# Attention values in blocks of eight heads, with twelve probability slots, in a one-core decoder layer

## The chip, the cores and the metric

The kernel runs on one core of a Trainium2 chip. The metric is the device time of one execution in microseconds (us), as the median of three runs. Lower is better.

## The reference

The input is a batch of 16 sequences of 256 tokens with 256 features, a second sequence of the same shape (the context), and a mask that is all ones. Three sub-layers follow one another, each added to its input and normalised over the features:

```
q, k, v = x @ w_qkv.T        # 16 heads of 16 features
q, k = rope(rms_norm(q)), rope(rms_norm(k))
x = layernorm(x + softmax(causal(q k^T / 4)) v @ w_proj.T)      # self attention
x = layernorm(x + softmax(causal((x Wq)(ctx Wk)^T / 4)) (ctx Wv) @ Wo)   # cross attention
x = layernorm(x + light_ffn(x) + heavy_ffn(x))  # gelu networks of 128 and 1024 hidden units
```

The heavy network is routed to 256 tokens of a sequence, and a sequence has 256, so it reaches every token. All arithmetic is at fp32 precision; where operands are narrower they are split into two or three terms.

## The kernel before, in words

All five engines run an instruction stream of their own, written out by hand as a loop of steps `i` from -2 to 19, and wait for one another by semaphores. A step works on four batches at once: self attention of batch `s = i`, cross attention of `c = i - 1`, the end of cross attention of `f = i - 2`, and the feed-forward network of `l = i - 3`. A whole step in the middle of the run has four phases on TensorE (PE), each a loop over 16 heads (`phase`), with other work put ahead of a given head by a dictionary `others` (constants such as `V2_AT`, at the end of the file):

- S1, scores of self attention (`scores(1, s, h)`): VectorE (DVE) takes the row maxima of each head (L1048).
- S2, scores of cross attention (`scores(2, c, h)`), the same.
- T1, transposed scores of self attention (`scores_t(1, s, h)`): ScalarE (ACT) takes the exponential of each head into a slot of `pr` (L854), GpSimd (POOL) masks it (L1433), and PE multiplies it with the values.
- T2, the same for cross attention.

The scores of all four phases go through a ring of three PSUM banks: PE may write head `h` only when DVE or ACT has read head `h - 3`. From the fourth step on, most heads of S1 and S2 find the mask already in their bank, written there by ACT (`write_bias`, L788 `bank<-cmaskb`); for the others PE adds it by a matmul (`cmaskb,idb`).

The values are taken four heads at a time (`values(a, b, gr)`, `a` = 1 for self, 2 for cross attention). The four heads lie side by side in PSUM bank 3, 32 partitions each, in columns 0 to 255, and each consists of two fp32 matmuls (256 and 128 columns), each of which the trace shows as two records; so a group is 16 records, `bank<-pr,va`. ACT then copies the group to `oT` (`copy_group`, 128x256), and the next group waits for that copy. `pr` has eight slots, so the exponential of head 8 waits for the values of heads 0 to 3, and so on. Groups 0, 1 and 2 stand ahead of heads 7, 11 and 15 of their phase, group 3 ahead of head 3 of the next phase: in T2 for self attention, in S1 of the next step for cross attention.

What stands around the groups: in T1, nine feed-forward matmul pairs (`FFN1_AT`, heads 0 to 10) and the transposes of `xn` ahead of head 8; in T2, `k2` ahead of head 1, the two halves of `qk1` ahead of heads 3 and 6, the self attention's output projection ahead of head 9, `v1` ahead of head 13. From that projection comes the first layer norm: DVE adds and takes statistics, POOL takes the inverse deviation between its masks of heads 12 and 13 (`RSTD1_AT`, L1412), DVE writes `x` (L1135), and PE transposes `x` ahead of head 1 of S1 (`transpose_x1`). Behind it in S1: the last cross values ahead of head 3, `q2` ahead of head 4, then `out_tokens`, `out_dims`, the cross output projection and the hidden layer. In S2, the transposes of the rotated q and k stand ahead of head 2 (`transpose_qk1`), those of the maxima ahead of head 4, `v2` ahead of head 6 (`V2_AT`), the feed-forward output from head 3 on.

ACT's order in S2, which the prediction comes back to: load of the exponential's table, copies of the two transposed halves, `xThigh`, bias writes for heads 6, 7 and 8, the copy of `v2`, bias for head 9, the copy of the context, bias for heads 10 to 15.

The rotation of q and k reads `qn` (the normalised and scaled pair, written by `scale_qk` on DVE in S1) and writes `qr`, which PE transposes in the following S2.

Of the kernel before, what the change touches and what calls it, by code (L numbers as in the profile page):

```python
# [43 lines left out]
P = 128  # L44
# [12 lines left out]
NG = H // HG  # L57
NB = T // VW
# [7 lines left out]
def build(nc, io):  # L66
# [4 lines left out]
    with ctx:  # L71
# [38 lines left out]
        qn = sb("qn", [P, TT, 2 * D]); rot = sq; qc = sb("qc", [P, TT, 2 * D]); qr = sb("qr", [P, TT, 2 * D])  # L110
# [15 lines left out]
        pr = sb("pr", [P, 2 * HG, 3 * P])  # L126
# [91 lines left out]
        def iterations(step):  # L218
            for i in range(-2, B + 4):
# [3 lines left out]
                 if 0 <= turn[2] < B]  # L223
        RING = (0, 1, 2)
# [174 lines left out]
        def _(pe):  # L399
# [98 lines left out]
            def hidden(b, j):  # L498
# [11 lines left out]
                elif b == B - 2:  # L510
# [7 lines left out]
                    elif j == 6:  # L518
                        pe.wait_ge(s_y[3], b)
                    elif j == LIGHT:  # L520
                        pe.wait_ge(s_oT[2], NG * B)
# [8 lines left out]
                elif j == 1:  # L530
                    pe.wait_ge(s_oT[2], NG * (b + 2))
# [42 lines left out]
            def transpose_max(a, b):  # L574
# [3 lines left out]
                else:  # L578
                    if live(b - 3):
                        pe.wait_ge(s_g, FCH * (b - 3) + LIGHT)  # L580
                    if live(b - 2):
                        pe.wait_ge(s_oT[2], NG * (b - 1))
                    wait(pe, s_oT[1], NG * b)
# [14 lines left out]
            def values(a, b, gr):  # L598

                pe.wait_ge(s_prob[a], H * b + HG * (gr + 1))  # L600
                if gr == 0:
# [3 lines left out]
                    elif live(b + 1):  # L605
                        pe.wait_ge(s_oT[1], NG * (b + 2))
                    elif live(b - 2):
                        pe.wait_ge(s_g, FCH * (b - 1))
                else:
                    pe.wait_ge(s_oT[a], NG * b + gr)  # L610
                v = values_of(a, b)
                for key in range(2):
                    for j in range(HG):
                        h = HG * gr + j
                        out = bank[OT_BANK][VW * j:VW * (j + 1), :]
                        if key == 0:
                            mm(out[:, 0:T], v[:, 0, h, :], pr[:, h % (2 * HG), 0:T], True, False, True)
                        else:
                            last = mm(out[:, P:T], v[:, 1, h, :], pr[:, h % (2 * HG), T:3 * P], False, True, True)
                last.then_inc(s_pv[a], 1)  # L620

            def out_tokens(b):

                pe.wait_ge(s_oT[2], NG * (b + 1))
# [74 lines left out]
            def step(i):  # L699
# [11 lines left out]
                if live(f):  # L711
                    add(OUT2_AT[0], values, 2, f, NG - 1)
# [62 lines left out]
                if live(c):  # L775
                    for gr in range(NG - 1):
                        add(HG * gr + VALUES_AFTER, values, 2, c, gr)
# [8 lines left out]
        def _(act):  # L786
# [3 lines left out]
            def copy_v(a, b):  # L790
                act.wait_ge(s_v[a], b + 1)

                wait(act, s_pv[a], NG * (b - 1) if a == 1 else NG * b)
# [12 lines left out]
            def copy_group(a, b, gr):  # L806
                act.wait_ge(s_pv[a], NG * b + gr + 1)
# [787 lines left out]
```

## Time and profile before

| | |
|---|---|
| median of 3 runs (lowest, highest) | 953.05 us (951.24, 955.12) |
| the profiled execution | 952.55 us, of which the trace's span is 950.8 us |
| PE busy | 852.0 us (90% of the span) |
| DVE busy | 720.1 us (76%) |
| ACT busy | 632.8 us (67%) |
| POOL busy | 538.7 us (57%) |
| mean granted TensorE clock | 0.969 |

Busy time is the time in which the engine had at least one instruction in work. PE's matmuls are pipelined and their ends are modelled, so its share is an upper figure, and for distances on PE the starts of two instructions are the safer measure. The granted clock is at full speed from the profile's ninth slice (of 40) to the end; before that some slices are at 60 to 80 per cent.

### The profile page before, as it was taken

Reading aid. Unit: us, or ns where it says so; the run is one execution under the profiler, and the core shown is the slowest. Engines: PE = TensorE matmul, PEld = TensorE weight load, DVE = VectorE, ACT = ScalarE, POOL = GpSimd, SP = SyncE. Lnnn points to the kernel's source line nnn. Section 1 sums busy time; section 2 is a strip of 40 time slices with the busy share of each in tenths; the row PEclk is TensorE's granted clock in tenths of the full one; section 3 lists DMA queues with packets and bytes.
Section 4 is the critical chain, followed back from the end, with each engine's and each line's share of the span. In section 5 each row is a group of like instructions: output and inputs, shape, how many; then the busy total and the mean of one; then the engine's idle time right before and its main releaser. Section 6 shows DMA issues by size and latency. Waiting matters only on the chain.

```text
span 950.8 us, 21384 instructions
## 1 busy us (share of the span) xinstructions
PE 852.0 (90%) x7381; PEld 649.0 (68%) x7381; DVE 720.1 (76%) x1765; ACT 632.8 (67%) x1404; POOL 538.7 (57%) x1047
## 2 busy tenths in 40 slices
PE   3367898999999999999999999999999999889887
PEld 2235565776867677776867676776867676657677
DVE  7788787787888878877888878877888879675522
ACT  1132453787878787787878778787878777776352
POOL 7554464656656574665756575655756665444143
PEclk8769898999999999999999999999999999999999
DMA  3794382845656382736676482826566472823101
GB/s 113 105 179 82 50 108 37 115 48 91 80 102 79 60 111 47 108 41 109 74 102 79 71 104 46 109 37 116 66 102 79 74 97 46 105 34 54 27 2 34
DMA packets 79660, 74.21 MB, mean 78 GB/s; under 512 B 8608, under 2 KB 78912, under 8 KB 79552
## 3 DMA queue, kind: packets, MB, share of 16 engines
q1 hardware_dynamic: 75024, 68.11, 50.7%
q10 hardware_dynamic: 4528, 4.73, 1.9%
q8 instruction: 59, 0.97, 0.5%
q14 instruction: 49, 0.40, 0.2%
HBM read 17.49 MB, written 4.20 MB: 23 GB/s over the span
## 4 chain that ended last, share of the span: by engine, by line
PE 60%; DVE 21%; ACT 5%; issue 5%; POOL 4%; DMA 3%; SPq 0%; ACTq 0%; POOLq 0%; DVEq 0%
PE bank L401 56%; DVE mx L1048 8%; PE bank L428 3%; POOL pr L1433 3%; DVE qn L1179 2%; ACT pr L854 2%; DVE x L1135 2%; ACT bank L788 1%; DMA stk2k<-nat1k 1%; POOL rstd L1412 1%; DVE y L1107 1%; DVE nt L1169 1%; ACT nat2q L788 1%; DVE rest L1022 1%; DVE st L1114 1%
## 5 line engine op out<-in xcount | busy, mean ns | idle before, releaser
L1433 POOL TENSOR_SCALAR_AFFINE_SELECT pr<-pr 128x256 f32<-128x256 f32 x512 | 223.1, 445 | 201.8 <-ACT pr L854 199.7
L854 ACT ACTIVATE pr<-bank 128x384 f32<-128x384 f32 x512 | 239.0, 495 | 138.2 <-PE bank L401 136.9
L1048 DVE TENSOR_REDUCE mx<-bank 128x3 f32<-128x384 f32 x512 | 264.5, 549 | 75.3 <-PE bank L401 70.6
L788 ACT ACTIVATE bank<-cmaskb 128x384 f32<-128x384 bf16 x331 | 155.0, 491 | 37.9 <-DVE mx L1048 33.0
L401 PE MATMUL bank<-w,g 128*128 128x256 f32 x576 | 171.2, 388 | 0.3 <-ACT g L874 0.3
L401 PE MATMUL bank<-stk2k,stk2q 97*128 97x128 bf16 (+1 forms) x512 | 87.2, 254 | 13.3 <-ACT bank L788 13.3
L401 PEld LDWEIGHTS bank<-w,g 128*128 128x128 f32 x576 | 89.3, 190 | 3.9 <-ACT g L874 0.7
L401 PE MATMUL bank<-stk1q,stk1k 100*128 100x256 bf16 (+1 forms) x512 | 79.2, 251 | 5.2 <-ACT pr L854 3.6
L874 ACT ACTIVATE g<-bank,b 128x256 f32<-128x256 f32 x144 | 65.1, 467 | 22.9 <-PE bank L401 22.9
L401 PE MATMUL bank<-stk1k,stk1q 97*128 97x128 bf16 (+1 forms) x512 | 75.4, 247 | 0.3 <-ACT bank L788 0.3
L401 PE MATMUL bank<-cmaskb,idb 128*128 128x256 bf16 x181 | 52.1, 288 | 25.0 <-DMA stk2k<-nat1k 13.9
L401 PE MATMUL bank<-stk2q,stk2k 100*128 100x256 bf16 (+1 forms) x512 | 70.3, 255 | 4.4 <-DMA stk2q<-mT 3.6
L401 PEld LDWEIGHTS bank<-stk2k,stk2q 97*128 97x128 bf16 x512 | 45.0, 100 | 42.5 <-ACT bank L788 25.6
L401 PE MATMUL bank<-xnh,w1h 128*128 128x256 f32 x288 | 66.9, 314 | 6.7 <-ACT g L874 6.5
L291 POOL TENSOR_TENSOR qc<-qn,ropeC 128x256 f32<-128x256 f32 x60 | 44.4, 741 | 43.4 <-DVE qn L1179 43.4
L401 PEld LDWEIGHTS bank<-stk1q,stk1k 100*128 100x128 bf16 x512 | 40.6, 99 | 40.0 <-ACT pr L854 11.7
L401 PE MATMUL bank<-wo,onT 128*128 128x256 f32 x256 | 63.2, 391 | 1.4 <-ACT onT L788 1.4
L1384 POOL TENSOR_SCALAR ve<-mv 128x2 f32<-128x2 f32 x47 | 10.4, 221 | 87.0 <-DVE mv L1120 85.7
L295 POOL TENSOR_TENSOR sq<-qn,ropeS 128x128 f32<-128x128 f32 x120 | 59.1, 514 | 0.0
L401 PEld LDWEIGHTS bank<-stk2q,stk2k 100*128 100x128 bf16 x512 | 36.7, 100 | 30.7 <-issue 14.5
L401 PE MATMUL bank<-xnh,w1l 128*128 128x256 f32 x288 | 57.6, 281 | 0.0
L401 PE MATMUL bank<-xnl,w1h 128*128 128x256 f32 x288 | 57.5, 281 | 0.0
(171 smaller groups left out, 1842.0 us busy)
## 6 DMA issues: line engine op xcount, KB each, us to landing
stk1q<-nat1q SPq DMA_DIRECT2D x90, 128.0 KB, 4.6
stk1k<-nat1k SPq DMA_DIRECT2D x90, 128.0 KB, 5.3
stk2k<-nat2k SPq DMA_DIRECT2D x90, 128.0 KB, 4.3
stk2q<-nat2q SPq DMA_DIRECT2D x90, 128.0 KB, 5.6
xT<-in_xT SPq DMA_DIRECT2D x16, 256.0 KB, 5.4
ctxT<-in_ctxT SPq DMA_DIRECT2D x16, 256.0 KB, 5.8
x<-in_x SPq DMA_DIRECT2D x16, 256.0 KB, 6.0
out_x<-x SPq DMA_DIRECT2D x15, 256.0 KB, 2.2
```

What stands on the lines that cost most here:

```text
L291: ops.tensor_tensor(qc[:, t, s * D:(s + 1) * D].rearrange("p (h d) -> p h d", d=HD), qn[:, t, s * D:(s + 1) * D].rearrange("p (h d) -> p h ...
L295: last = ops.tensor_tensor(rv[:, s, :, half, :], qv[:, s, :, 1 - half, :], ropeS[:, t, s:s + 1, half * h2:(half + 1) * h2] .to_broadcast([ ...
L401: return nc.tensor.matmul(out, lhsT, rhs, start=start, stop=stop, skip_group_check=check)
L428: last = nc.tensor.transpose(bank[k][:, c * T + t * P:c * T + (t + 1) * P], src[:, t, c * P:(c + 1) * P], idf[:, :])
L788: return nc.scalar.activation(out, in_, ACT.Copy)
L854: nc.scalar.activation(pr[:, h % (2 * HG), :], ring_bank("T", a, b, h)[:, 0:3 * P], ACT.Exp, scale=HD ** -0.5)\
L874: nc.scalar.activation(g[:, j, :], hidden_out(b, j), ACT.Gelu, bias=b1[:, j:j + 1])\
L1048: V.tensor_reduce(mx3[:, h, :], scored[:, 0:3 * P].rearrange("p (k t) -> p k t", k=3), AX.X, ALU.max, negate=True).then_inc(s_mx[a], 1)
L1135: V.tensor_scalar(xo[a][:, t, :], y[a][:, t, :], mv[a][:, t, 0:1], rstd[a][:, t:t + 1], ALU.subtract, ALU.mult).then_inc(s_x[a], 1)
L1179: V.tensor_tensor(qn[:, t, :].rearrange("p (h d) -> p h d", d=HD), bank[QK1_BANK[t]][:, :].rearrange("p (h d) -> p h d", d=HD), rr[:, t, : ...
L1384: G.tensor_scalar(ve[a][:, :], mv[a][:, :, 1], LN_EPS, None, ALU.add).then_inc(s_ve[a], 1)
L1433: G.affine_select(out=slot, in_=slot, compare_op=ALU.is_ge, fill=0.0, base=0, pattern=[[0, 2], [1, P]], channel_multiplier=-1).then_inc(s_ ...
```

## The change

Values are taken eight heads at a time. The second four heads go to columns 256 to 511 of the same bank, without the start flag, and one copy of 128x512 takes both to `oT`. Half 0 stands ahead of head 11 of its phase (`VALUES_AT`), half 1 where group 3 stood, ahead of head 3 of the next phase. `pr` grows from eight to twelve slots, used in turn over all heads of all phases; an exponential waits for the half that last read its slot. The memory for that comes from `qr`, which becomes another name for `qn`; `scale_qk` now waits for the transposes of the batch before instead of its rotation. `v2` moves from head 6 to head 1 of S2, past the transposes of q and k, those of the maxima, and two feed-forward pairs. All waits that counted four groups count two halves.

```diff
-        qn = sb("qn", [P, TT, 2 * D]); rot = sq; qc = sb("qc", [P, TT, 2 * D]); qr = sb("qr", [P, TT, 2 * D])
+        qn = sb("qn", [P, TT, 2 * D]); rot = sq; qc = sb("qc", [P, TT, 2 * D]); qr = qn
-        pr = sb("pr", [P, 2 * HG, 3 * P])
+        pr = sb("pr", [P, SLOTS, 3 * P])
...
+        transposed = [turn[1:] for turn in turns if turn[0] == "T"]
+        def slot(a, b, h):
+            return (H * transposed.index((a, b)) + h) % SLOTS
...
-            def values(a, b, gr):
-                pe.wait_ge(s_prob[a], H * b + HG * (gr + 1))
-                if gr == 0:
+            def values(a, b, half):
+                pe.wait_ge(s_prob[a], H * b + HV * (half + 1))
+                if half == 0:
...
-                    pe.wait_ge(s_oT[a], NG * b + gr)
+                    pe.wait_ge(s_oT[a], NV * b + half)
                 for key in range(2):
-                    for j in range(HG):
-                        h = HG * gr + j
-                        out = bank[OT_BANK][VW * j:VW * (j + 1), :]
+                    for j in range(HV):
+                        h = HV * half + j
+                        n = slot(a, b, h)
+                        out = bank[OT_BANK][VW * (j % HG):VW * (j % HG + 1), j // HG * T:(j // HG + 1) * T]
                         if key == 0:
-                            mm(out[:, 0:T], v[:, 0, h, :], pr[:, h % (2 * HG), 0:T], True, False, True)
+                            mm(out[:, 0:T], v[:, 0, h, :], pr[:, n, 0:T], j < HG, False, True)
...
-                    for gr in range(NG - 1):
-                        add(HG * gr + VALUES_AFTER, values, 1, s, gr)
+                    add(VALUES_AT, values, 1, s, 0)
...
-                    add(OUT1_AT[0], values, 1, s, NG - 1)
+                    add(OUT1_AT[0], values, 1, s, 1)
...
-                copy(oT[:, gr, :], bank[OT_BANK][:, 0:T]).then_inc(s_oT[a], 1)
+                copy(oT[:, PG * half:PG * (half + 1), :], bank[OT_BANK][:, :].rearrange("p (g t) -> p g t", g=PG))\
+                    .then_inc(s_oT[a], 1)
...
-                if h >= 2 * HG:
-                    act.wait_ge(s_pv[a], NG * b + h // HG - 1)
...
+                n = H * transposed.index((a, b)) + h - SLOTS
+                if n >= 0:
+                    a0, b0 = transposed[n // H]
+                    act.wait_ge(s_pv[a0], NV * b0 + n % H // HV + 1)
...
-                if live(f):
-                    copy_group(2, f, NG - 2)
...
-                    copy_group(2, f, NG - 1)
+                    copy_half(2, f, 1)
...
-                        if h % HG == 0 and h >= 2 * HG:
-                            copy_group(1, s, h // HG - 2)
+                        if h == SLOTS:
+                            copy_half(1, s, 0)
                         exponential(1, s, h)
...
-                        if h % HG == 0 and h >= 2 * HG:
-                            copy_group(2, c, h // HG - 2)
+                        if h == SLOTS:
+                            copy_half(2, c, 0)
                         exponential(2, c, h)
...
             def scale_qk(b, t):
                 dve.wait_ge(s_new, NEWTON * (b + 1))
-                wait(dve, s_rope, TT * b)
+                wait(dve, s_nat[1], 2 * b)
...
-VALUES_AFTER = 7
+VALUES_AT = 11
-QKT_AT, MAX1_AT, V2_AT = 2, 4, 6
+QKT_AT, MAX1_AT, V2_AT = 2, 4, 1
```

## Rows read from the trace of the kernel before

**Rows 1.** The page's fourth part: the chain that ended last, by engine.

```profile
PE 60%; DVE 21%; ACT 5%; issue 5%; POOL 4%; DMA 3%; SPq 0%; ACTq 0%; POOLq 0%; DVEq 0%
```

**Rows 2.** Timeline of PE, T1 and T2: start, duration (us), instruction, [idle before <-releaser].

```profile
481.20 0.33 PE L401 MATMUL bank<-stk1q,stk1k 100*128 100x256 bf16 x2
481.46 0.86 PE L401 MATMUL bank<-pr,va1a 128*32 128x256 f32 x16
...
485.67 0.67 PE L401 MATMUL bank<-stk1q,stk1k 100*128 100x256 bf16 x6
486.59 0.34 PE L401 MATMUL bank<-stk1q,stk1k 100*128 100x256 bf16 x2 [0.25 <-ACT pr L854]
487.06 0.86 PE L401 MATMUL bank<-pr,va1a 128*32 128x256 f32 x16
487.85 0.34 PE L401 MATMUL bank<-stk1q,stk1k 100*128 100x256 bf16 x2
488.02 0.33 PE L401 MATMUL bank<-stk2q,stk2k 100*128 100x256 bf16 x2
...
490.90 0.73 PE L401 MATMUL bank<-wqk1high,xThigh 128*128 128x512 f32 x2
...
498.77 0.50 PE L401 MATMUL bank<-stk2q,stk2k 100*128 100x256 bf16 x4
```

**Rows 3.** Timeline of ACT in the same T1.

```profile
484.72 0.59 ACT L788 ACTIVATE xnh<-bank 128x512 fp32r<-128x512 f32 x1
485.19 0.50 ACT L854 ACTIVATE pr<-bank 128x384 f32<-128x384 f32 x1
486.04 0.49 ACT L854 ACTIVATE pr<-bank 128x384 f32<-128x384 f32 x1 [0.35 <-PE bank L401]
...
486.69 1.26 ACT L854 ACTIVATE pr<-bank 128x384 f32<-128x384 f32 x3
```

**Rows 4.** The chain in order of time, from T2 into S1: start, duration, what.

```profile
500.36 0.41 POOL pr L1433
...
501.79 0.89 DVE x L1135 x2
...
511.19 1.33 PE bank L401 x10
```

**Rows 5.** Timeline of PE at the start of the S1 that follows.

```profile
502.74 0.66 PE L428 MATMUL bank<-idf,x 128*128 128x128 f32 x4 [0.30 <-DVE x L1135]
...
503.88 0.86 PE L401 MATMUL bank<-pr,va 128*32 128x256 f32 x16
504.80 0.28 PE L401 MATMUL bank<-cmaskb,idb 128*128 128x256 bf16 x1
...
505.09 1.89 PE L401 MATMUL bank<-x1T,wq 128*128 128x256 f32 x8
506.82 0.33 PE L401 MATMUL bank<-stk1k,stk1q 97*128 97x128 bf16 x2
```

**Rows 6.** Timeline of PE in S2, just ahead of that T1.

```profile
465.95 0.34 PE L401 MATMUL bank<-stk2k,stk2q 97*128 97x128 bf16 x2
467.00 0.34 PE L401 MATMUL bank<-stk2k,stk2q 97*128 97x128 bf16 x2 [0.71 <-ACT bank L788]
467.18 1.04 PE L428 MATMUL bank<-idf,qr 128*128 128x128 f32 x8
...
470.17 0.48 PE L401 MATMUL bank<-wv2high,ctxhigh 128*128 128x256 f32 x2
...
471.66 0.34 PE L401 MATMUL bank<-stk2k,stk2q 97*128 97x128 bf16 x2
```

**Rows 7.** Timeline of ACT in the same S2.

```profile
470.62 1.32 ACT L788 ACTIVATE bank<-cmaskb 128x384 f32<-128x384 bf16 x3
...
472.63 0.49 ACT L788 ACTIVATE bank<-cmaskb 128x384 f32<-128x384 bf16 x1 [0.18 <-DVE mx L1048]
...
473.58 3.19 ACT L788 ACTIVATE bank<-cmaskb 128x384 f32<-128x384 bf16 x6
```

More of the change, by code:

```diff
@@ L57 @@
 NG = H // HG
+NV = 2
+HV = H // NV
+SLOTS = 12
 NB = T // VW
@@ L530, in hidden @@
                 elif j == 1:
-                    pe.wait_ge(s_oT[2], NG * (b + 2))
+                    pe.wait_ge(s_oT[2], NV * (b + 2))
                 else:
@@ L581, in transpose_max @@
                     if live(b - 2):
-                        pe.wait_ge(s_oT[2], NG * (b - 1))
-                    wait(pe, s_oT[1], NG * b)
+                        pe.wait_ge(s_oT[2], NV * (b - 1))
+                    wait(pe, s_oT[1], NV * b)
                 for t in range(TT):
@@ L711, in step @@
                 if live(f):
[L712 removed]
+                    add(OUT2_AT[0], values, 2, f, 1)
                 if live(c):
@@ L775, in step @@
                 if live(c):
-                    for gr in range(NG - 1):
-                        add(HG * gr + VALUES_AFTER, values, 2, c, gr)
+                    add(VALUES_AT, values, 2, c, 0)
                 phase((lambda h: scores_t(2, c, h)) if live(c) else None, others)
@@ L791, in copy_v @@
                 act.wait_ge(s_v[a], b + 1)
-                wait(act, s_pv[a], NG * (b - 1) if a == 1 else NG * b)
+                wait(act, s_pv[a], NV * (b - 1) if a == 1 else NV * b)
                 copy(values_of(a, b)[:, :, :, 0:HD], bank[V_BANK[a]][:, :].rearrange("p (t h d) -> p t h d", t=TT, h=H))\
@@ L804, in copy_out, with copy_half @@
                 copy_dims(onT[2], dim_bank(b)).then_inc(s_onT[2], 1)
-            def copy_group(a, b, gr):
-                act.wait_ge(s_pv[a], NG * b + gr + 1)
+            def copy_half(a, b, half):
+                act.wait_ge(s_pv[a], NV * b + half + 1)
                 if a == 1:
@@ L812, in copy_group @@
                 elif live(b + 1):
-                    act.wait_ge(s_tok, C * (b + 1) + gr // PG + 1)
+                    act.wait_ge(s_tok, C * (b + 1) + half + 1)
                 else:
                     wait(act, s_ott, TT * b)
-                copy(oT[:, gr, :], bank[OT_BANK][:, 0:T]).then_inc(s_oT[a], 1)
+                copy(oT[:, PG * half:PG * (half + 1), :], bank[OT_BANK][:, :].rearrange("p (g t) -> p g t", g=PG))\
+                    .then_inc(s_oT[a], 1)
             def copy_x1(b):
@@ L843, in exponential @@
                 act.wait_ge(s_st[a], H * b + h + 1)
-                if h >= 2 * HG:
-                    act.wait_ge(s_pv[a], NG * b + h // HG - 1)
-                elif a == 1:
-                    wait(act, s_pv[2], NG * (b - 1) - 2 + h // HG + 1)
-                    wait(act, s_pv[1], NG * b)
-                elif live(b + 1):
-                    act.wait_ge(s_pv[1], NG * (b + 1) + 3 + h // HG)
-                else:
-                    act.wait_ge(s_pv[2], NG * (b - 1) + 3 + h // HG)
-                nc.scalar.activation(pr[:, h % (2 * HG), :], ring_bank("T", a, b, h)[:, 0:3 * P], ACT.Exp, scale=HD ** -0.5)\
+                n = H * transposed.index((a, b)) + h - SLOTS
+                if n >= 0:
+                    a0, b0 = transposed[n // H]
+                    act.wait_ge(s_pv[a0], NV * b0 + n % H // HV + 1)
+                nc.scalar.activation(pr[:, slot(a, b, h), :], ring_bank("T", a, b, h)[:, 0:3 * P], ACT.Exp, scale=HD ** -0.5)\
                     .then_inc(s_exp[a], 1)
@@ L1431, in mask_probs @@
                     wait_apart(pool, (s_exp[a], H * b + h + 1))
-                    slot = pr[:, h % (2 * HG), :].rearrange("p (k t) -> p k t", t=P)[:, 0:3:2, :]
-                    G.affine_select(out=slot, in_=slot, compare_op=ALU.is_ge, fill=0.0, base=0,
+                    probs = pr[:, slot(a, b, h), :].rearrange("p (k t) -> p k t", t=P)[:, 0:3:2, :]
+                    G.affine_select(out=probs, in_=probs, compare_op=ALU.is_ge, fill=0.0, base=0,
                                     pattern=[[0, 2], [1, P]], channel_multiplier=-1).then_inc(s_prob[a], 1)
```

14 lines of the change are left out of this document (6 added, 8 removed).

## The prediction

> **What bounds the kernel now.** I read the chain of waits first, over the whole span and then over one period, then PE's timeline in that period, then ACT's. Over the span the chain lies on PE for 60% and on DVE for 21% [rows 1]. Over one period the reader is to see where it changes hands. In T1 and T2 it is PE. Near the end of T2 it leaves PE: an exponential, POOL's masks, its inverse deviation, then DVE's `x` at 501.79, the rest of DVE's root iterations and the first maxima of S1, until at 511.19 a hidden-layer matmul that waited for the last links of that row (DVE, ACT) takes it back to PE [rows 4]. At the end of S1 it passes DVE and an ACT bias write, and the second head of S2 finds PE idle [rows 6]. So PE's own time counts where the chain is on PE, and a saving just ahead of `x` or of that bias write is lost in a wait. I replay one middle period against these rows: S2 at 466, T1 at 477, T2 at 488, S1 at 502.
>
> **What joining two blocks saves.** A four-head block starts 0.26 us after the head before it (481.20 to 481.46), where a head follows a head after 0.17 (487.85 to 488.02); the next matmul starts 0.79 after the block (487.06 to 487.85) [rows 2]. Eight records of 256 fp32 columns take 505.09 to 506.82, 0.216 each [rows 5]; four heads side by side have two records of 256 and two of 128 columns after one another, so 2 x 0.216 + 2 x 0.108 = 0.65. A block thus costs 0.09 ahead and 0.14 behind its streaming: joining two saves 0.23. There are 16 batches x 2 attentions x 2 pairs = 64 pairs, 14.7 us of PE's queue. The eight-head block is in no row: its distance to the next matmul is 0.79 + 0.65 = 1.44 if the second four heads stream on, and at most 2 x 0.79 + 0.09 = 1.67 if the seam costs as much as two blocks do. I take 1.44, since inside the old block the second key's weights follow the first's without such a gap.
>
> **T1.** Without the block ahead of head 7, everything from there comes 0.88 earlier (0.79 + 0.09). The first half starts at 484.00 (old second block: 484.88, which is head 11's 485.67 less 0.79), its mask long done, and head 11 at 485.44 instead of 485.67. Heads 11, 12 and 13 go at once, as now (three records of two at 485.67) [rows 2]. From here PE has only scores to issue until the next phase, and the ring lets head 14 go when exponential 11 is read: 0.37 from head 11 to its exponential (485.67 to 486.04), 0.55 from there to head 14 (486.59) [rows 2, 3], so 486.36. Then the copy stands ahead of exponential 12. Exponentials follow one another after 0.39 (three in 1.26 with a last one of 0.49 [rows 3]); from exponential 11 to the next there are 0.65 now, so the 128x256 copy costs ACT 0.26. A copy of 128x512 costs 0.47 (484.72 to 485.19 [rows 3]). Exponential 12 starts at 485.81 + 0.39 + 0.47 = 486.67, head 15 at 487.22, and T2's first head, behind exponential 13, at 487.61. In the old order the third block filled this hole: PE stood still for 0.42 ahead of head 14 and 0.21 ahead of the block; now for 0.42, 0.69 and 0.22. That is 0.70 more, against 0.46 saved on two joins by the second half's end.
>
> **T2.** From its first head to `qk1` there are 2.88 (488.02 to 490.90 [rows 2]) with one block inside; with the longer one 3.53, so 491.14, 0.24 later than now. Then the block ahead of head 7 goes (-0.88) and the one ahead of head 11 grows (+0.65): head 11 at 498.78, against 498.77 [rows 2]. Up to here three joins saved 0.69 and the new idle time took it back: nothing won, nothing lost.
>
> **The layer norm's link.** ACT's copy ahead of exponential 12 is again 0.47 instead of 0.26, and POOL's mask 12, the inverse deviation behind it and `x` follow: +0.21, `x` from 502.00. PE reaches the transposes of `x` early, since the block ahead of head 15 is gone (0.88), and waits: they start at 502.95 instead of 502.74. The trace has PE waiting for `x` there already [rows 5].
>
> The Trainium skill, Perfetto Trace Analysis, section Optimizing Scalar/DVE Operations, speaks against this part of the change: if ScalarE or VectorE are not saturated but cause bubbles on other engines, breaking up instructions may let work finish sooner. ACT is such an engine here and the change joins its copies; the two spacings above agree with the rule. By it alone the period would be 0.21 longer, 2.9 us over 14 periods.
>
> **S1.** Now the half ahead of head 3 has eight heads: it starts at 504.09 instead of 503.88, and head 3 follows at 505.53 instead of 504.80 [rows 5]; 0.13 of the old 0.92 was a wait for the first maxima, now covered. So +0.73, and head 4 behind `q2` goes from 506.82 to 507.55 [rows 5]. From there `out_tokens`, DVE's division, ACT and gelu lead to the matmul at 511.19, which already waits [rows 4]. DVE's side alone would come 0.21 later, but it needs head 4's scores and `out_tokens`; I carry +0.7 to the end of S1. Bounds: +0.21 (all absorbed by that wait) and +0.73.
>
> **S2.** PE issues its first head at 465.95 and the second at 467.00: 0.88 idle. `v2` takes 1.49 (470.17 to 471.66) [rows 6], and at head 1 it fills that hole, so PE could be 0.88 ahead from head 6 on. But the bias writes of heads 6 to 15 are ACT's, and between 470.62 and 473.58 ACT's only hole is 0.18 [rows 7]; what stands ahead of 470.62 does not move. Heads 10 to 15 can come 0.18 earlier and no more. Passing the transposes of q, k and maxima, `v2` makes these later by 1.49 less the hole, 0.6: DVE needs the transposed maxima before its fourth reduction, and bias 6 needs that reduction; this eats into PE's lead, not into ACT's row. As for the wait ahead of `v2` (its bank, read by the second residual), everything behind it on PE would wait too; that read ends before the last maxima of S1. Bounds: -0.88 and +0.1; I take -0.18, which rows 7 set.
>
> **At nothing.** `qn` in place of `qr`: the transposes that read it start at 467.18 [rows 6], and DVE writes it again after `x` of 501.79 [rows 4], 33 us later; were that cover gone, DVE would stall in S1. Twelve slots and the waits on them: each half read its slot a phase earlier, except exponentials 12 to 15, whose half PE issues ahead of head 11. The slots' memory sets no time.
>
> **Sum.** Per period 0.00 + 0.70 - 0.18 = +0.52; 14 periods (batches 1 to 14, all four phases present): +7.3. At the very end the last half has four heads more (0.65) and a longer copy (0.21), with its last mask some 0.4 earlier: +0.4. From the profiled execution's 952.55 this is 960.2; the median shown is 953.05, 0.5 above it, within the spread of the three. I say 960.
>
> **Rivals.**
> - *The hole in S2 is recovered whole.* If ACT's copies between its bias writes slide forward (the table load ahead of them ends early enough), S2 gives 0.88: +0.70 - 0.88 = -0.18, 14 times -2.5, so 950. For it: the idle 0.71 that the trace itself shows at the second head [rows 6]. Against: ACT's single hole [rows 7].
> - *Faster: the waits give way at `x`.* Place: the transposes at head 1 of S1. If `x` comes as early as PE does, some 1.2 us earlier, all four joins of a period count and so does S2: -0.92 - 0.18 = -1.10, 14 times -15.4, so 937. It decides from `x` ready before 501.8. For it: the output projection comes 0.65 earlier in T2. Against: POOL takes the inverse deviation only behind mask 12 [rows 4], and exponential 12 does not come earlier. The Trainium skill has the rule behind this rival (TensorEngine Tiling, Array Packing, Key Properties): changing the tiling mode drains TensorE. The 0.09 and 0.14 agree; by that rule alone the 64 joins give 14.7 us, 938.
> - *Slower still: the seam costs what a block costs.* Then each half is 0.23 longer: three on the way to head 12 of T2 (+0.69) and one in S1 (+0.23), 1.44 a period, 20 us, so 973. Against: the streaming inside the old block.
> - *The change doesn't do what it says:* if the second four heads waited for the first (one bank), it would look like the last one.
>
> **How the numbers follow.** Forecast 0.45 (own range 955 to 966), S2 whole 0.25 (946 to 954), faster 0.17, seam 0.13. About 0.5%, 4.8 us, can be told from no change. Faster by more (below 948.3): the third and a quarter of the second, 0.22. Within: the rest of the second and a fifth of the first, 0.28. Slower (above 957.8): 0.36 of the first, and the last, 0.50. Range 938 to 970: it leaves out about half of the faster case and half of the seam's.
>
> **What would show it.** Right: blocks of 32 records, 1.44 from start to next; in T1 a wait of PE for `pr` ahead of head 15; POOL's mask 12 with a 128x512 copy two places ahead of it; PE idle over 1 us for `x`; no hole at S2's second head but waits for ACT's bias later; a period about 0.5 longer. Wrong: `x` earlier relative to T1's first head, head 10 of S2 more than 0.3 earlier, a block over 1.5, or a PE that does not wait in T1.

## The result, and the profile after

The kernel after takes 974.78 us (median; 973.24 to 975.32), the kernel before beside it 953.17: a ratio of 1.0224 (95% interval 1.0200 to 1.0248), that is 2.2% slower. The forecast was 960, with a range of 938 to 970: the direction was right, the size was outside the range. The profiled execution took 974.52 us (span 972.8; before 950.8), at a mean granted clock of 0.955 (before 0.969).

From the page of the kernel after, the busy rows and the chain by engine:

```profile
PE 854.7 (88%) x7381; PEld 659.2 (68%) x7381; DVE 721.3 (74%) x1765; ACT 622.8 (64%) x1340; POOL 545.3 (56%) x1047
...
PE 56%; DVE 16%; ACT 13%; issue 7%; POOL 4%; DMA 3%; SPq 0%; ACTq 0%; POOLq 0%; DVEq 0%
```

PE's work has hardly changed; what grew is the share of the chain on ACT, from 5% [rows 1] to 13%. PE's timeline in one T1 and T2 of the kernel after, the counterpart of [rows 2 and 5]:

```profile
486.93 0.33 PE L409 MATMUL bank<-stk1q,stk1k 100*128 100x256 bf16 x2
...
493.47 1.51 PE L409 MATMUL bank<-pr,va1a 128*32 128x256 f32 x32
494.91 0.67 PE L409 MATMUL bank<-stk1q,stk1k 100*128 100x256 bf16 x6
495.83 0.34 PE L409 MATMUL bank<-stk1q,stk1k 100*128 100x256 bf16 x2 [0.25 <-ACT pr L857]
496.70 0.34 PE L409 MATMUL bank<-stk1q,stk1k 100*128 100x256 bf16 x2 [0.53 <-ACT pr L857]
497.18 0.33 PE L409 MATMUL bank<-stk2q,stk2k 100*128 100x256 bf16 x2
...
511.15 0.27 PE L409 MATMUL bank<-cmaskb,idb 128*128 128x256 bf16 x1 [0.34 <-ACT pr L857]
...
512.51 0.65 PE L436 MATMUL bank<-idf,x 128*128 128x128 f32 x4 [0.93 <-DVE x L1134]
...
513.65 1.51 PE L409 MATMUL bank<-pr,va 128*32 128x256 f32 x32
515.09 0.28 PE L409 MATMUL bank<-cmaskb,idb 128*128 128x256 bf16 x1
```

The block of 32 records runs 1.44 from its start to the next matmul (493.47 to 494.91), so its halves stream on. Head 15 of T1 waits for `pr` a second time, and the transposes of `x` wait 0.93 behind an earlier 0.34. ACT in the same T1 shows why head 15 waits (rows 3 are its counterpart): the 128x512 copy sits between exponentials 11 and 12.

```profile
495.29 0.49 ACT L857 ACTIVATE pr<-bank 128x384 f32<-128x384 f32 x1 [1.00 <-PE bank L409]
495.67 0.59 ACT L795 ACTIVATE oT<-bank 128x512 f32<-128x512 f32 x1
496.15 2.03 ACT L857 ACTIVATE pr<-bank 128x384 f32<-128x384 f32 x5
```

The same copy stands in T2 ahead of exponential 12, and from there the chain goes on as in [rows 4]. First ACT's timeline, then the chain in order of time:

```profile
509.10 0.59 ACT L795 ACTIVATE oT<-bank 128x512 f32<-128x512 f32 x1
509.57 0.50 ACT L857 ACTIVATE pr<-bank 128x384 f32<-128x384 f32 x1
```

```profile
510.14 0.41 POOL pr L1432
510.55 0.20 POOL ve L1383
...
510.82 0.72 POOL rstd L1411
...
511.57 0.90 DVE x L1134 x2
...
512.51 0.65 PE bank L436 x4
```

S2 in PE's timeline, the counterpart of [rows 6]: `v2` fills the old hole behind the first head, and the waits for ACT's bias writes come later and smaller.

```profile
475.57 0.34 PE L409 MATMUL bank<-stk2k,stk2q 97*128 97x128 bf16 x2
475.67 0.48 PE L409 MATMUL bank<-wv2high,ctxhigh 128*128 128x256 f32 x2
...
477.16 0.34 PE L409 MATMUL bank<-stk2k,stk2q 97*128 97x128 bf16 x2
...
480.84 0.34 PE L409 MATMUL bank<-stk2k,stk2q 97*128 97x128 bf16 x2 [0.28 <-ACT bank L795]
...
486.31 0.34 PE L409 MATMUL bank<-stk2k,stk2q 97*128 97x128 bf16 x2 [0.26 <-ACT bank L795]
```

**Where the 22 us lie.** PE transposes `x` once per batch, so these starts mark off the span. Span differences to the kernel before, in us; the last column is from the sixteenth transposes to the end of the span:

```
                          to 1st  1st-2nd  2nd-14th (12)  14th-15th  15th-16th  to end   sum   middle period
after                      +1.07    +4.28      +7.25        +2.75      +4.04    +2.61   +22.0   53.80
after, copy late (e12)     +1.04    +2.95      -6.13        +0.16      +0.99    +1.99    +1.0   52.82
copy late in ends (e13)    +0.75    +2.93      +4.73        +0.15      +1.00    +1.94   +11.5   53.79
copy late in middle (e14)  +2.61    +3.41      -3.67        +1.12      +3.59    +1.14    +8.2   52.80
fours in the ends (e5)     +0.75    +1.70      +7.55        +0.32      +0.40    +0.08   +10.8   53.80
```

The period was 53.20 before. So a third of the loss is in the middle, at +0.60 a period (forecast +0.52); 14.75 us are in the first two and last three columns taken together, for which the forecast had 1.4 (two of its 14 periods and the +0.4). In e13 the twelve intervals take in end steps too: nearly all of the 2.5 by which its column lies under that of the kernel after is in the first of them (50.23, after 52.22) and the last (53.34, after 53.83). The kernels of the other rows are told below.

### The profile page after: what moved, and what is told of

It reads as the page before. It is cut to its first block, busy times and chain, and to the rows that moved or that the text cites. A ratio compares the mean times of both kernels' runs of the same rounds, so it can differ in the third digit from the quotient of the medians.

```text
span 972.8 us, 21190 instructions
## 1 busy us (share of the span) xinstructions
PE 854.7 (88%) x7381; PEld 659.2 (68%) x7381; DVE 721.3 (74%) x1765; ACT 622.8 (64%) x1340; POOL 545.3 (56%) x1047
## 4 chain that ended last, share of the span: by engine, by line
PE 56%; DVE 16%; ACT 13%; issue 7%; POOL 4%; DMA 3%; SPq 0%; ACTq 0%; POOLq 0%; DVEq 0%
PE bank L409 53%; DVE mx L1047 6%; ACT bank L795 4%; PE bank L436 3%; POOL pr L1432 3%; ACT pr L857 2%; DVE x L1134 2%; DMA stk2k<-nat1k 1%; ACT oT L795 1%; POOL rstd L1411 1%; DVE y L1106 1%; ACT nat2q L795 1%; DVE rest L1021 1%; ACT L916 1%; DVE rden L1094 1%
## 5 line engine op out<-in xcount | busy, mean ns | idle before, releaser
L1432 POOL TENSOR_SCALAR_AFFINE_SELECT pr<-pr 128x256 f32<-128x256 f32 x512 | 230.3, 462 | 204.4 <-ACT pr L857 202.5
L857 ACT ACTIVATE pr<-bank 128x384 f32<-128x384 f32 x512 | 229.8, 499 | 146.5 <-PE bank L409 146.5
L409 PE MATMUL bank<-stk1k,stk1q 97*128 97x128 bf16 (+1 forms) x512 | 77.5, 252 | 0.3 <-ACT bank L795 0.3
L299 POOL TENSOR_TENSOR qc<-qn,ropeC 128x256 f32<-128x256 f32 x60 | 49.4, 823 | 46.7 <-DVE qn L1178 46.7
L409 PE MATMUL bank<-stk2q,stk2k 100*128 100x256 bf16 (+1 forms) x512 | 65.7, 254 | 7.2 <-DMA stk2q<-mT 3.3
L303 POOL TENSOR_TENSOR sq<-qn,ropeS 128x128 f32<-128x128 f32 x120 | 53.9, 470 | 0.0
```

Of the source, the lines that this page charges most:

```text
L299: ops.tensor_tensor(qc[:, t, s * D:(s + 1) * D].rearrange("p (h d) -> p h d", d=HD), qn[:, t, s * D:(s + 1) * D].rearrange("p (h d) -> p h ...
L303: last = ops.tensor_tensor(rv[:, s, :, half, :], qv[:, s, :, 1 - half, :], ropeS[:, t, s:s + 1, half * h2:(half + 1) * h2] .to_broadcast([ ...
L409: return nc.tensor.matmul(out, lhsT, rhs, start=start, stop=stop, skip_group_check=check)
L857: nc.scalar.activation(pr[:, slot(a, b, h), :], ring_bank("T", a, b, h)[:, 0:3 * P], ACT.Exp, scale=HD ** -0.5)\
L1432: G.affine_select(out=probs, in_=probs, compare_op=ALU.is_ge, fill=0.0, base=0, pattern=[[0, 2], [1, P]], channel_multiplier=-1).then_inc( ...
```

## The experiments

Times are medians, ratios are to the kernel before on the same chip with their 95% interval. "Period" is the distance of one transposition of `x` to the next in the middle.

**e1, e2, e3: parts alone.** e1 is the kernel before with `v2` early:

```diff
-QKT_AT, MAX1_AT, V2_AT = 2, 4, 6
+QKT_AT, MAX1_AT, V2_AT = 2, 4, 1
```

> The kernel before with one part of the change alone: v2 ahead of head 1 of S2. My theory (ACT's row of copies and bias writes sets heads 10 to 15 of S2): the period falls by about 0.2 us, 953 to 950.5 (0.26%). Rival (PE's hole of 0.88 us is recovered whole): the period falls by 0.9, to 941. A third (the transposes of q and k and of the maxima, pushed back by 0.6, hold up what follows): no gain or slower, 953 to 958.

952.55, ratio 0.9996 (0.9985 to 1.0007). The period fell to 53.04, by 0.16, where [rows 7] gave 0.18: ACT's bias writes are the limit and the hole of 0.88 is not recovered whole. The profiled execution lost 0.77 between the first two marks, 0.50 between the last two and 1.11 behind them, so the time stayed.

e2 is the kernel after with that same line put back:

> The changed kernel with v2 back ahead of head 6. My theory: the period is 0.2 us longer than the changed kernel's, 974.8 to 977. Rival (v2's move is worth the whole hole): 987. Third (the move is what cost): below 974.

972.40, ratio 1.0212 (1.0190 to 1.0235); the period is 53.95, 0.15 longer, so in the middle the part is additive. The time is not the theory's 974.8 to 977; it lies where the third theory had it, below 974. But the six executions spread from 969.31 to 976.69 (the profiled one took 976.50), so over all no effect of the part can be told.

e3 is the kernel before with blocks of four, but twelve slots and `qr = qn`:

```diff
-        pr = sb("pr", [P, 2 * HG, 3 * P])
+        pr = sb("pr", [P, SLOTS, 3 * P])
...
-                wait(dve, s_rope, TT * b)
+                wait(dve, s_nat[1], 2 * b)
```

> The kernel before with twelve slots and the rotated q and k in the scaled ones' memory, but values still four heads at a time, and v2 where it was. My theory: neither the slots' waits nor the shared memory set any time, 953 within 1 us. Rival (the new wait of the scaling on the transposes, or the later reuse of a slot, holds something up): over 956.

951.94, ratio 0.9999 (0.9989 to 1.0010), period 53.2. The slots and the shared memory cost nothing, as forecast.

**e4: is it the clock?** The granted clock has two levels here, 2.4 and 1.2 GHz. In the profiled executions the time at 1.2 GHz rose from 58.1 us before to 87.9 after: 10 us of that in the first steps, 20 behind the fourteenth transposes, where the kernel before stays at 2.4 GHz. e4 adds PE work without use in the first and last steps (the part for the scores):

```diff
+                if (a, b) in FILLED:
+                    for _ in range(2):
+                        mm(out[:, 0:T], kk[0:K_ALL, h, 0:P], q[0:K_ALL, h, :], True, False, True)
```

> The changed kernel with extra TensorE work that no result needs, only in the first two steps and the last two: each transposed score of these phases is preceded by two copies of its first matmul into the same bank, and six matmuls of constants stand ahead of four of the transposes of x, ten ahead of two late transposes. Clock theory (of the 22 us lost, some 14 were lost in these steps because TensorE idled there and the chip then granted half its clock, 90 us of half clock against 60): the half-clock time falls by 15 us or more and the run is faster in spite of more work, 966 to 970. Rival (the larger blocks' waits themselves cost these 14 us, the clock follows from them): no gain, 974 to 980.

973.73, ratio 1.0225 (1.0213 to 1.0238). The time at 1.2 GHz fell to 46.9 us and the mean granted clock rose to 0.976, and the time stayed. As a remedy, keeping the clock up is refuted; that the lower clock contributes is not excluded, since the added work takes PE's time too (e16 comes back to it).

**e5: blocks of four in the end batches.** A function chooses the block for each attention `a` and batch `b`:

```diff
+def eight(a, b):
+    return 2 <= b < 13
```

> The kernel after, but with eight heads to a block only in batches 2 to 12; batches 0, 1, 13, 14 and 15 go by blocks of four as the kernel before did (slots, copies, output order of those batches too). Theory A (the larger blocks cost 0.60 us in each middle period, by the distances of the transposes of x, and the other 14 us of the 22 arise in the first two and last three batches because nothing else stands on PE there while a block waits for its masks): the middle period stays at 53.80, the last interval from the transposes of x to the end falls from 82.6 to about 80.0, the two before it from 54.3 to about 51.6 and 50.3, and the time is 959 to 962. Rival B (the end intervals are long for a reason that does not hang on the size of the blocks there, for example the twelve slots, the place of v2 or a state carried over from the middle batches): the intervals stay within 0.5 of those of the kernel after and the time is 972 to 975. A part each (v2's earlier place kept here cost 0.8 at the start and 1.6 at the end when it was made alone): 961 to 965.

962.14, ratio 1.0095 (1.0074 to 1.0116): 12.6 us came back and the middle stayed at 53.80. The last intervals are theory A's (51.91, 50.66 and 80.11); the time lies just over A's 962, in the range given for a part each. Of the 14.75 us at the ends 3.25 remained, so most of that loss, not all, comes with the joined blocks.

**e6, e7, e8: which attention, and T1's hole.** The same function with `a == 1` (e6) and `a == 2` (e7); e8 is e6 with two feed-forward groups moved:

```diff
-FFN1_AT = (0, 1, 2, 3, 4, 6, 8, 9, 10)
+FFN1_AT = (0, 1, 2, 3, 4, 6, 8, 14, 15)
```

> The kernel after, but eight heads to a block only in the self attention (T1 and the first half of T2); the cross attention (T2's end, S1, S2) goes by blocks of four. Replay by the prediction's terms: T1 and T2 to qk1 +0.24 (forecast; +0.32 measured in the kernel after), the block ahead of T2's head 7 is then there again, S1's block is a small one (-0.73 against the kernel after), v2's place -0.16. Theory A (most of the middle period's +0.60 is S1's longer block ahead of head 3): the period is 53.2 to 53.4, that is 0.4 to 0.6 under the kernel after, and the time 958 to 964, since T1's hole without filler also stands in the first and last batches. Rival B (the loss is T1's hole alone): the period stays at 53.7 to 53.8 and the time is above 970.

> The kernel after, but eight heads to a block only in the cross attention; the self attention goes by blocks of four, as before. Theory A (S1's longer block is the middle period's loss): +0.73 at S1, -0.16 for v2, about -0.02 to -0.2 at x: a period of 53.5 to 53.75 and a time of 960 to 967. Rival B (T1's hole is the loss): the period is 53.0 to 53.2 and the time within 0.5% of the kernel before. The steps at the start and end tell which attention's blocks cost the 14 us there: if the intervals of the last two batches stay at 54.3 it is the cross attention's, if they fall to 51.6 and 50.3 the self attention's.

> The self-only version, with two feed-forward groups of TensorE work moved from T1's later heads (9 and 10) to the places ahead of heads 14 and 15, where the larger block leaves PE idle for the ring. Theory A (joining two blocks saves 0.23 each and T1's idle time ahead of heads 14, 15 and of T2's first head takes it back): with that hole filled the period is 0.5 to 0.8 under the self-only version, 52.5 to 52.8, and the time 5 to 10 us under it. Rival B (the hole is set by ACT's exponentials and copy, and the moved groups only shift PE's idle time to the ring earlier in T1, or their results come too late for the next step's use): the same time as the self-only version within 2 us, or more.

e6: 962.54, ratio 1.0100 (1.0077 to 1.0122), period 53.37, both inside A's ranges and below B's. e7: 959.49, 1.0071 (1.0044 to 1.0098), period 53.49, a trifle below A's figures and well above B's. Against e1's 53.04, which has `v2` early too, they are +0.33 and +0.45, and both together (53.80) +0.76: the two parts add up. From the first mark to the second most of the loss is the self attention's: +4.32 there for e6, +1.39 for e7. The sign that e7 was to give for the last batches came out mixed: its last two full intervals are 52.79 and 52.13, those of e6 51.39 and 53.06 (after 54.34 and 54.30, before 51.59 and 50.26), so neither attention has that loss alone. e8: 954.61, 1.0023 (1.0009 to 1.0038), period 52.79: filling T1's hole gives 0.58 a period, so the hole was real and joined blocks pay once it is filled. The start of the kernel after, PE's timeline of the first T1 (no other work of a batch on PE), shows the self attention's loss:

```profile
59.60 4.27 PE L409 MATMUL bank<-stk2q,stk2k 100*128 100x256 bf16 x22 [3.31 <-DMA stk2q<-mT]
68.67 2.79 PE L409 MATMUL bank<-pr,va1a 128*32 128x256 f32 x32 [4.80 <-POOL pr L1432]
```

POOL's timeline at the same place, first the eleven masks together, then the seventh and the eighth, each asked for alone:

```profile
60.70 8.99 POOL L1432 TENSOR_SCALAR_AFFINE_SELECT pr<-pr 128x256 f32<-128x256 f32 x11 [1.91 <-ACT pr L857]
...
64.42 1.52 POOL L1432 TENSOR_SCALAR_AFFINE_SELECT pr<-pr 128x256 f32<-128x256 f32 x1
...
65.90 2.72 POOL L1432 TENSOR_SCALAR_AFFINE_SELECT pr<-pr 128x256 f32<-128x256 f32 x1
```

DVE's timeline there, two instructions that split a weight once at the start:

```profile
64.23 1.45 DVE L1194 CAST w1h<-g 128x2304 fp32r<-128x2304 f32 x1
65.71 2.64 DVE L1196 TENSOR_TENSOR w1l<-g,w1h 128x2304 fp32r<-128x2304 f32 x1
```

and the kernel before, PE's timeline, with the block that there needs four masks only:

```profile
63.06 1.51 PE L401 MATMUL bank<-pr,va1a 128*32 128x256 f32 x16 [1.03 <-POOL pr L1433]
...
68.11 1.51 PE L401 MATMUL bank<-pr,va1a 128*32 128x256 f32 x16 [2.02 <-POOL pr L1433]
```

Eight masks come before the larger block. They took 8.2 together: the seventh and the eighth ran beside the two DVE instructions and ended 0.26 and 0.27 behind them, the other six took 0.40 to 0.89 each. The ring has nothing to issue meanwhile, and PE stands 4.80 at one place instead of 1.03 and 2.02 at two (before the second of these the eighth mask took 2.46, beside the same DVE instruction).

**e9 to e11: putting it together.** e9 is the kernel before with twelve slots (and `qr = qn`); in the middle steps alone it has the self attention in eights, T1's hole filled, and `v2` early:

```diff
+    return a == 1 and 3 <= b < 15
...
-                    add(V2_AT, v2, c)
+                    add(V2_AT if 1 <= c < 14 else V2_END, v2, c)
...
-                        add(FFN1_AT[j], ffn_out, l, 1, j)
+                        add((FFN1_FILL if eight(1, s) else FFN1_AT)[j], ffn_out, l, 1, j)
```

> The kernel before (blocks of four, v2 ahead of head 6) with twelve slots, and in the middle steps alone three parts of what was learned: eight heads to a block in the self attention of batches 3 to 14, two feed-forward groups in T1's hole ahead of heads 14 and 15 there, v2 ahead of head 1 of S2 for batches 1 to 13. Theory A (the middle period of the self-only version with the hole filled was 0.41 under the kernel before; what it lost was the first three and last batches, +6.1 by the third transposes of x and +2.7 in the last interval but one): the same period of 52.79, intervals at both ends within 0.5 of the kernel before, 947 to 949. Rival B (the ends pay for any shorter middle, since the steps there wait for something that does not move): 951 to 953.

948.12, ratio 0.9960 (0.9947 to 0.9974), period 52.77, as theory A had it; the profiled execution is the fastest of the five, at 944.61. e10 moves ACT's copies behind the exponentials that others wait for:

```diff
-COPY_HALF_AT = 12
+COPY_HALF_AT = 14
+COPY_FOUR_AT = {8: 0, 13: 1}
```

> The version of e9 with ACT's copies moved behind the exponentials that others wait for: the self attention's 128x512 copy from ahead of exponential 12 to ahead of 14, the cross attention's second 128x256 copy from ahead of exponential 12 to ahead of 13 (all batches). Theory A (the chain to x runs through exponential 12, mask 12, the inverse deviation; the copy ahead of it costs the spacing of 0.26): x 0.26 earlier, a period of 52.4 to 52.6 and 943 to 946. Rival B (PE's arrival at the transposes of x, not x, sets the period once T1's hole is filled, as PE waits there only 0.30): the period is 52.7 to 52.8, the time within 1 us of e9.

941.70, ratio 0.9882 (0.9867 to 0.9897), period 52.07: 0.70 less, about twice what A gave, and the time under A's range. From T1's first head to T2's first it is 0.46 less (9.21, in e9 9.67), which A had left out, and from there to `x` 0.18 less. e11 has the cross attention in eights too (batches 3 to 13):

> The version of e10 with eight heads to a block in the cross attention too, batches 3 to 13; its 128x512 copy stands ahead of exponential 14. Theory A (what the cross attention's larger block cost, 0.29 with v2's gain of 0.16 in it, is S1's longer block ahead of head 3, 0.73, less the wait it covers; the copy is out of the way): 0.2 to 0.5 a period over e10, 945 to 951. Rival B (with the copy behind exponential 12 x comes early enough that the joined blocks ahead of heads 7 and 15 of T2 count): 0.1 to 0.5 a period under e10.

945.99, ratio 0.9929 (0.9914 to 0.9945), period 52.26: +0.19, a little under A's bound; its sign is A's.

**e12: the place of the copy alone.** The kernel after with one change, made in the form of e5 with `eight` always true:

```diff
-                        if h == SLOTS:
-                            copy_half(1, s, 0)
+                        if eight(1, s) and h == COPY_HALF_AT:
+                            copy_block(1, s, 0)
...
+COPY_HALF_AT = 14
```

(and the same for the cross attention).

> The kernel after with one change: ACT's 128x512 copy stands ahead of exponential 14 instead of 12, in both attentions. Theory A (the terms of the forecast: 0.47 of copy ahead of exponential 12 delays heads 15 of T1 and the first head of T2, and in T2 mask 12, the inverse deviation and x): PE's waits ahead of T1's head 15 and for x get 0.4 to 0.5 shorter, a period of 52.9 to 53.4 instead of 53.80, and 961 to 969. Rival B (the period is set elsewhere, by S1's block and by S2's bias writes): 53.7 to 53.8 and 972 to 975.

955.71, ratio 1.0032 (1.0020 to 1.0045): 19.1 us of the 21.6 are gone, more than theory A allowed. PE's timeline of T1 and T2, to be read beside the one above:

```profile
478.11 0.33 PE L416 MATMUL bank<-stk1q,stk1k 100*128 100x256 bf16 x2
...
487.02 0.72 PE L416 MATMUL bank<-stk1q,stk1k 100*128 100x256 bf16 x4 [0.25 <-ACT pr L868]
487.87 0.33 PE L416 MATMUL bank<-stk2q,stk2k 100*128 100x256 bf16 x2
...
502.71 0.66 PE L443 MATMUL bank<-idf,x 128*128 128x128 f32 x4 [0.42 <-DVE x L1153]
```

ACT's timeline there, the copy behind three exponentials:

```profile
486.47 1.26 ACT L868 ACTIVATE pr<-bank 128x384 f32<-128x384 f32 x3 [1.00 <-PE bank L416]
487.60 0.62 ACT L804 ACTIVATE oT<-bank 128x512 f32<-128x512 f32 x1
```

The wait of 0.53 ahead of head 15 is gone, and the one for `x` is 0.42 instead of 0.93. From T1's first head to T2's first it is 9.76 instead of 10.25, from there to `x` 14.84 instead of 15.33: 0.49 each, 0.98 a period. That is about the copy's spacing of 0.47 twice.

**e13, e14: the same move in the ends or the middle alone.** The copy stands ahead of exponential `12 if 2 <= b < 13 else 14` in e13, the other way round in e14.

> The kernel after, with ACT's 128x512 copy ahead of exponential 14 instead of 12 in batches 0, 1, 13, 14 and 15 alone. Theory A (in the end steps, too, the copy's place is the larger part of the loss: with the copy late everywhere they lost 5.3 us instead of 15.4): middle period 53.80 as in the kernel after, the last two intervals 51.5 to 52 instead of 54.3, the time 963 to 967. Rival B (in the end steps the larger block itself, which waits for eight masks, is the loss, and the late copy's 10 us there came from the shorter middle handed on): intervals at the ends within 0.7 of the kernel after, 971 to 975.

> The kernel after, with the copy ahead of exponential 14 in batches 2 to 12 alone. Theory A: middle period 52.82 (0.98 less, eleven times: 10.8 us), ends as in the kernel after, 962 to 966. Rival B (the ends' gain came from the shorter middle): ends short as well, 955 to 958. The savings of e13 and e14 should add up to the 19.0 of the run with the copy late everywhere, within 2 us.

e13: 966.35, ratio 1.0137 (1.0117 to 1.0157), 8.4 less than the kernel after, as theory A had it. e14: 960.74, 1.0081 (1.0062 to 1.0099), 14.0 less, of which eleven periods at 0.98 are 10.8; A had the ends unchanged, 962 to 966. The two add up to 22.4, 3.3 more than e12's 19.1, so they are not independent: in the table the last three columns of e14, whose copies stand as in the kernel after, sum to +5.9 instead of +9.4. Rival B has that part. The trace shows something of how: in these three columns the mean granted clock was 0.97, 0.91 and 0.96 in the kernel after and 1.00, 0.91 and 0.99 in e14, and 3.10 of the 3.55 lie in the first and the third, where the clock differs.

**e15: the copy in the kernel before.** The second 128x256 copy of each attention ahead of exponential 13 (the same edit for `1, s`):

```diff
-                        if h % HG == 0 and h >= 2 * HG:
-                            copy_group(2, c, h // HG - 2)
+                        if h in (8, 13):
+                            copy_group(2, c, h // 13)
```

> The kernel before with its second 128x256 copy of each attention ahead of exponential 13 instead of 12. Theory A (every exponential that waits behind a copy ahead of 12 costs the copy's spacing: at x 0.26; in T1 the third block fills the hole, so little there): x 0.2 to 0.3 earlier a period, 52.9 to 53.0, and 948 to 950. Rival B (mask 12 and the inverse deviation do not set x in the kernel before once PE's own work is counted): 53.1 to 53.2, 951 to 953.5.

957.20, ratio 1.0042 (1.0025 to 1.0059), 0.4% slower; period 53.21, as before. Theory A missed what waits for the copy: in T1 the next block of four needs the bank that it reads. PE's timeline:

```profile
489.81 0.86 PE L401 MATMUL bank<-pr,va1a 128*32 128x256 f32 x16 [0.41 <-ACT oT L788]
...
490.77 0.33 PE L401 MATMUL bank<-stk2q,stk2k 100*128 100x256 bf16 x2
...
505.31 0.66 PE L428 MATMUL bank<-idf,x 128*128 128x128 f32 x4
```

`x` no longer waits (14.54 from T2's first head, before 14.72), but T1 is 0.28 longer (10.86, before 10.58). With eight heads to a block no block follows the copy inside a phase, so it can be late; in T1 blocks of four pay for it. This explains the unchanged period, not the slower time: of the 4.9 us that the profiled execution lost, 0.5 are in the twelve middle intervals, 2.15 ahead of the second mark and 2.20 in the last three columns. No run takes these apart.

**e16: the best version.** e10 with the cross attention's late copy in batches 2 to 14 alone:

```diff
+                        if not eight(2, c) and h in COPY_FOUR_AT[2 <= c < 15]:
...
-COPY_FOUR_AT = {8: 0, 13: 1}
+COPY_FOUR_AT = ({8: 0, 12: 1}, {8: 0, 13: 1})
```

> The version of e10 with the cross attention's late copy in batches 2 to 14 alone (ahead of 12 in 0, 1 and 15). Theory A (the late copy cost e10 the 4.5 us that it lost against e9 by the third transposes of x): period 52.07 as in e10, the third transposes of x at 181 to 183 instead of 185.7, and 936 to 940. Rival B (that loss comes from when the clock fell and rose in the first steps of one execution): 940 to 943.

938.24 (937.94 to 941.76), ratio 0.9854 (0.9832 to 0.9875): it beats both kernels. The period is 52.07 as in e10; the third transposes start at 182.0, as theory A had it. The rival is not excluded with that, since the profile also shows 6.8 us less at 1.2 GHz up to there than e10's.

The profiled execution is the slowest of the four (941.76), and it shows what the clock costs. From the fifteenth to the sixteenth transposes its code is that of e10, but it takes 53.38 instead of 50.48 there. The mean granted clock of this interval is 0.94, with two stretches at 1.2 GHz, 6.8 us together; in e10 it is 1.00. One place of it in PE's timeline, first e10, then e16:

```profile
840.90 0.63 PE L443 MATMUL bank<-idf,xn 128*128 128x128 f32 x4 [0.27 <-DVE mT L1087]
841.37 0.66 PE L416 MATMUL bank<-stk1q,stk1k 100*128 100x256 bf16 x6
```

```profile
838.40 1.08 PE L443 MATMUL bank<-idf,xn 128*128 128x128 f32 x4 [0.27 <-DVE mT L1087]
839.28 1.17 PE L416 MATMUL bank<-stk1q,stk1k 100*128 100x256 bf16 x6
```

PE's waits ahead of the first stretch are the same in both. Set beside e10, PE is 1.58 behind after the first stretch, still 1.58 when the second begins, and 2.90 behind after it. So in the last steps the clock alone can take 2.90, with the same instructions.

## Why the prediction was wrong

**T1 and T2: right.** The replay put T2's first head 10.17 behind T1's (measured 10.25, before 10.58), and `x` 15.34 behind that (measured 15.33, before 14.72). The new idle time is where it was put, ahead of T1's head 15, and e12 shows that it is the copy's: 0.49 in T1 and 0.49 at `x`, from the forecast spacing of 0.47. The Trainium skill (Perfetto Trace Analysis, Optimizing Scalar/DVE Operations) would break up an instruction of an engine that is not saturated but makes others idle; the trace agrees on the bubble, and e12 removed 0.98 a period of it by the place of the copy alone, without breaking it up.

**S1 and S2: right.** From `x` to the next T1 the forecast had 0.70, less the 0.21 that `x` already carries, less 0.18, that is +0.31; measured +0.33 (28.22, before 27.89). S1's block takes 1.44 (513.65 to 515.09), `v2` gives 0.16 (e1).

**The block, the slots: right.** The rival of the costly seam is refuted by the 1.44, although its 973 lies nearest to the result; its time was right for a wrong reason. The rival with S2's hole whole is refuted by e1. The rival with the waits giving way was refuted for this kernel, but e12 shows that the copy is what keeps it from happening: with it late, the joins show in part (the rival had 1.10 a period) and the period is 0.38 under the kernel before.

**The sum: the step that failed.** "14 periods" at +0.52 and "+0.4" at the very end treated the steps at both ends like the middle, or as free. Measured: +7.25 for the twelve intervals in between, of the forecast size (0.60 each), and +14.75 in the first two and last three columns of the table. The terms of the middle came from a replay in which other work stands on PE while a block waits for its masks. At the start that cover is missing (eight masks, 4.80 of idle, in the first T1 above). In the last steps T2 has no `qk1` and no `v1`; in the kernel after, PE's timeline of the step ahead of the fifteenth transposes:

```profile
822.08 1.51 PE L409 MATMUL bank<-pr,va1a 128*32 128x256 f32 x32
...
824.68 1.10 PE L409 MATMUL bank<-stk2q,stk2k 100*128 100x256 bf16 x6 [0.50 <-ACT pr L857]
826.39 3.30 PE L409 MATMUL bank<-wo,onT 128*128 128x256 f32 x8 [0.60 <-DVE onT L1088]
...
830.25 1.51 PE L409 MATMUL bank<-pr,va 128*32 128x256 f32 x32
...
833.49 0.34 PE L409 MATMUL bank<-stk2q,stk2k 100*128 100x256 bf16 x2 [0.53 <-ACT pr L857]
```

and in e12, the copy late:

```profile
811.18 1.97 PE L416 MATMUL bank<-wo,onT 128*128 128x256 f32 x8 [0.60 <-DVE onT L1107]
...
813.40 1.51 PE L416 MATMUL bank<-pr,va 128*32 128x256 f32 x32
```

Each wait that the middle hides stands open. From the last self block to `x` this step takes 13.79 (822.08 to 835.87), in e12 11.68 (806.86 to 818.54), in the kernel before 11.02 (809.50 to 820.52). The difference of 2.11 to e12 has two parts. The output projection and the scores behind it take 3.86 (826.39 to 830.25), in e12 2.22 (811.18 to 813.40): 1.64, in a stretch at 1.2 GHz that e12 has not. The other 0.48 is the wait of 0.53 ahead of the last head, which the late copy removes. The same wait of 0.53 stands in T1, ahead of the fall of the clock. Whether it brought the clock down is not shown: e10 and e16 have different clocks behind the same waits.

Over all, e13 puts 8.0 of the 14.75 in the profiled executions on the copy's place, and e5 puts 11.5 on the joined blocks as such, copies and all. Both include what the clock did: the time at 1.2 GHz was 87.9 us in the kernel after, 59.9 in e13 and 70.9 in e5. The forecast had no term for the clock. An estimate from e16 (2.90 for 6.8 us) puts some 7 of the 9.4 us in the last three columns on the 17 us at 1.2 GHz that the kernel after has between 827 and 909. e4 can't confirm it, since its added work raises PE's busy time by 9.7. What stays open: how much of the loss at the ends would be left at the same clock, and how much of the start is the moment at which the clock rises, since the first marks differ by up to 2 us between kernels that are the same there.

So the mistake was one of scope. The timeline of the kernel before shows that its first step waits for masks already (1.03 and 2.02), and the forecast replayed one period only.

## What to carry to other kernels

When a change makes a unit of work larger, replay a period of the middle and also the first and last steps, where nothing covers the wait for its input, and look at the granted clock there. When two copies are joined, look at what stands behind the copy on its engine: here the larger copy's place, ahead of two exponentials that others waited for, cost more than joining blocks saved, and moving it by two places gave 19 of 22 us back. A larger block loosens an order (no block waits for the copy any more), and that freedom has to be used for the change to pay.

## What the runs showed of the hardware

Raising the granted clock from 0.955 to 0.976 (41 us less at 1.2 GHz) with extra PE work changed the time by 1.1 us only (e4). Without extra work, 6.8 us at 1.2 GHz made one interval of the last steps 2.90 longer than the same instructions took at 2.4 GHz (e16, e10). POOL's masks of one shape mostly took 0.41 each in the middle (`510.14 0.41` above); in the first T1 those that ran beside a DVE instruction over 128x2304 took 1.52 and 2.72 and ended 0.26 and 0.27 behind it, in the kernel before 2.46 and 0.27. That they waited for DVE is read from these three; no run moved the DVE instructions.
